# Loading x in one transfer per 256-token chunk, without VectorE's wait ahead of the statistics

## The reference, cut to what matters

```python
def bitlinear(x, W):
    sw = jnp.mean(jnp.abs(W)) + 1e-05
    Wq = jnp.clip(jnp.round(W / sw), -1.0, 1.0) * sw
    sx = 127.0 / jnp.clip(jnp.max(jnp.abs(x), axis=-1, keepdims=True), 1e-05, None)
    xq = jnp.clip(jnp.round(x * sx), -128.0, 127.0) / sx
    return jnp.einsum('bsd,od->bso', xq, Wq)
...
xn = _layernorm(x, axis=-1)
# attention: q (16 heads of 128), k and v (4 heads) by bitlinear, rope on q and k,
# causal softmax, output by bitlinear
x = x + attn(xn, Wq, Wk, Wv, Wo) + ffn(xn, gate_w, up_w, down_w, gate_s, up_s, down_s)
```

## Time and profile before

| | us |
|---|---|
| the two runs shown | 5373.88 and 5649.85 |
| their median | 5511.86 |
| the profiled execution | 5373.28 |
| span of its slowest core (core 2), first to last instruction | 5371.7 |
| spans of its eight cores | 5334.6 to 5371.7 |

### The profile page before, as it was taken

How to read it: one execution, slowest core, us unless ns; L and a number is a source line. 1 busy time by engine, 2 the same in 40 slices (tenths; PEclk the granted TensorE clock), 3 DMA queues, 4 the chain that set the end, 5 groups by cost and what they waited for, 6 DMA issues and landing times.

```text
span 5371.7 us, 55820 instructions; the slowest of 8 cores (5334.6 to 5371.7 us)
## 1 busy us (share of the span) xinstructions
PE 3815.0 (71%) x18728; PEld 1766.5 (33%) x18728; DVE 1706.2 (32%) x2837; ACT 1637.1 (30%) x1375; POOL 303.1 (6%) x276
## 2 busy tenths in 40 slices
PE   1799998979999898144445044545788989993188
PEld 1344444434444344133333033433222222222133
DVE  4211110111100000455555465665422111117533
ACT  4211110001111000533332622121455656663521
POOL 0111110101111010000000000000000000000000
PEclk9999999989999999566667576778999999995589
DMA  4999999999988697311110501101000000000366
GB/s 131 82 112 109 115 99 106 118 106 113 112 79 78 65 99 97 116 53 53 51 53 16 149 32 47 50 32 50 14 10 8 8 7 6 6 5 0 102 192 208
DMA packets 1048274, 387.69 MB, mean 72 GB/s; under 512 B 882240, under 2 KB 1025984, under 8 KB 1035712
## 3 DMA queue, kind: packets, MB, share of 16 engines
q0 software_dynamic: 548608, 161.50, 29.8%
q1 hardware_dynamic: 499392, 222.62, 18.3%
HBM read 480.53 MB, written 41.94 MB: 97 GB/s over the span
## 4 chain that ended last, share of the span: by engine, by line
PE 53%; DVE 19%; DMA 13%; ACT 9%; issue 5%; DVEq 1%; SPq 0%; ACTq 0%; POOLq 0%; POOL 0%
PE f_pd_h L389 10%; PE f_pg_h L343 9%; PE f_pu_h L349 8%; PE e_po L1018 4%; PE c_pse L811 3%; PE c_ppv L815 3%; ACT c_pp L869 2%; PE c_psc L860 2%; PE c_psc L858 2%; PE c_pse L813 2%; PE c_ppv L817 2%; PE b_pkv L625 2%; DVE b_mx L169 2%; DMA pp_wb<-wv_t 2%; DVE c_pp L878 2%
## 5 line engine op out<-in xcount | busy, mean ns | idle before, releaser
L869 ACT ACTIVATE c_pp<-c_psc 128x1024 bf16<-128x1024 f32 x640 | 654.7, 1023 | 583.8 <-PE c_psc L860 583.8
L343 PE MATMUL f_pg_h<-xnT,f_gw_h 128*128 128x512 bf16 x2816 | 628.5, 382 | 56.4 <-DMA f_uw_h<-uw_t 50.5
L389 PE MATMUL f_pd_h<-hdnT,f_dw_h 128*128 128x512 bf16 x2816 | 616.7, 381 | 46.4 <-DMA f_dw_h<-dw_t 44.1
L349 PE MATMUL f_pu_h<-xnT,f_uw_h 128*128 128x512 bf16 x2816 | 622.1, 379 | 0.0
L878 DVE TENSOR_TENSOR c_pp<-c_pp,cmask 128x512 bf16<-128x512 bf16 x512 | 217.8, 425 | 798.8 <-ACT c_pp L869 769.9
L726 PE MATMUL b_pq<-b_xqT,qtern 128*128 128x256 bf16 x2048 | 277.0, 297 | 244.6 <-DVE b_qrot L735 235.9
L343 PEld LDWEIGHTS f_pg_h<-xnT,f_gw_h 128*128 128x128 bf16 x2816 | 276.7, 98 | 394.1 <-issue 66.9
L389 PEld LDWEIGHTS f_pd_h<-hdnT,f_dw_h 128*128 128x128 bf16 x2816 | 275.9, 98 | 376.7 <-issue 53.4
L349 PEld LDWEIGHTS f_pu_h<-xnT,f_uw_h 128*128 128x128 bf16 x2816 | 275.5, 98 | 332.3
L603 PE MATMUL b_pkv<-b_xqT,ktern 128*128 128x256 bf16 x1024 | 180.9, 359 | 285.8 <-DVE b_krot L612 269.0
L811 PE MATMUL c_pse<-c_pp,c_onehot 128*16 128x512 bf16 x640 | 245.0, 383 | 133.9 <-DVE c_pp L878 127.7
(11 more groups left out here) (160 smaller groups left out, 3588.8 us busy)
## 6 DMA issues: line engine op xcount, KB each, us to landing
f_gw_h<-gw_t POOLq DMA_DIRECT2D x88, 512.0 KB, 9.2
f_uw_h<-uw_t POOLq DMA_DIRECT2D x88, 512.0 KB, 13.4
f_dw_h<-dw_t POOLq DMA_DIRECT2D x32, 1408.0 KB, 18.9
b_xch<-x_kv SPq DMA_DIRECT2D x32, 1024.0 KB, 6.8
f_xch<-x_q SPq DMA_DIRECT2D x4, 4096.0 KB, 17.0
pp_wb<-wq_t SPq DMA_DIRECT2D x64, 256.0 KB, 12.0
ffn_scr<-f_ffs_h SPq DMA_DIRECT2D x32, 512.0 KB, 5.1
pp_wb<-wo_t SPq DMA_DIRECT2D x64, 256.0 KB, 12.0
```

The costliest lines, as they stand in the source:

```text
L343: e.matmul(pg[:, bi, tc * 512:(tc + 1) * 512], gwb[wb][:, dt, :], xnT[:, dt, half * HT + tc * 512: half * HT + (tc + 1) * 512], start=(dt ...
L349: e.matmul(pu[:, bi, tc * 512:(tc + 1) * 512], uwb[wb][:, dt, :], xnT[:, dt, half * HT + tc * 512: half * HT + (tc + 1) * 512], start=(dt ...
L389: e.matmul(pd[:, pb, tc * 512:(tc + 1) * 512], dwb[wb][:, it, :], hdnT[:, it, tc * 512:(tc + 1) * 512], start=(it == 0), stop=(it == NIT - 1))
L869: E("scalar", lambda e, k0=k0, sbk=sbk: e.activation(pp[:, (k0 % 8):(k0 % 8) + 2, :].rearrange("p a b -> p (a b)"), psc[sbk][:], AF.Exp, s ...
```

## The change

For each chunk of B1 and B2 the two loads of 128 rows become one load of 256 rows into both halves of the tile, with one semaphore, for which both row sums and both sums of squares wait. The semaphores of the second halves go, and `emit_ln` takes one wait for all its tiles (stage F did so before). VectorE's separate wait for `xqT_pe[0]` ahead of the statistics goes too. Bytes moved, buffers and all arithmetic stay.

```diff
--- before.py
+++ after.py
@@ -82,8 +82,6 @@
     s_const = sem("s_const")
     s_x = [sem("s_x0"), sem("s_x1")]
     s_xb = [sem("s_xb0"), sem("s_xb1"), sem("s_xb2")]
-    s_xc = [sem("s_xc0"), sem("s_xc1"), sem("s_xc2")]
-    s_x2 = [sem("s_x20"), sem("s_x21")]
     s_rope = [sem("s_rope0"), sem("s_rope1")]
     s_mask = sem("s_mask")
     s_wb = [sem("s_wb0"), sem("s_wb1")]
@@ -134,14 +132,13 @@
 
     def emit_ln(xch, stats, wait_load, per_tile_fn=None):
         nt = stats["nt"]
-        wl = wait_load if isinstance(wait_load, list) else [wait_load] * nt
         sm, ssq_, mmean, rstd, nbias = (stats[k] for k in ("sm", "ssq", "m", "rstd", "nb"))
         for t in range(nt):
             E("vector", lambda e, t=t: e.reduce_sum(sm[:, t:t + 1], xch[:, t, :], AX.X),
-              waits=[wl[t], (ve, ve.n)], inc=(ve, 1))
+              waits=[wait_load, (ve, ve.n)], inc=(ve, 1))
             E("scalar", lambda e, t=t: e.activation(stats["junk"][:], xch[:, t, :],
                                                     AF.Square, accum_out=ssq_[:, t:t + 1]),
-              waits=[wl[t], (ac, ac.n)], inc=(ac, 1))
+              waits=[wait_load, (ac, ac.n)], inc=(ac, 1))
         vw, aw = ve.n, ac.n
         E("vector", lambda e: e.tensor_scalar(mmean[:], sm[:], 1.0 / D, None, ALU.mult),
           waits=[(ve, vw), (ac, aw)], inc=(ve, 1))
@@ -551,15 +548,11 @@
                 for c in range(NCH):
                     cb = c % 2
                     cb3 = c % 3
-                    ldw0 = (s_xb[cb3], s_xb[cb3].n + 16)
-                    ldw1 = (s_xc[cb3], s_xc[cb3].n + 16)
-                    ldw = [ldw0, ldw1]
+                    ldw = (s_xb[cb3], s_xb[cb3].n + 16)
                     E("sync", lambda e, c=c, cb3=cb3: e.dma_start(
-                        out=xch[:, cb3, 0, :], in_=x_kv[c * 256:c * 256 + 128, :]),
+                        out=xch[:, cb3, :, :], in_=x_kv[c * 256:(c + 1) * 256, :]
+                        .rearrange("(t p) f -> p t f", p=128)),
                       waits=[(ve, xch_done[cb3][0]), (ac, xch_done[cb3][1])], inc=(s_xb[cb3], 16))
-                    E("sync", lambda e, c=c, cb3=cb3: e.dma_start(
-                        out=xch[:, cb3, 1, :], in_=x_kv[c * 256 + 128:(c + 1) * 256, :]),
-                      waits=[(ve, xch_done[cb3][0]), (ac, xch_done[cb3][1])], inc=(s_xc[cb3], 16))
                     E("gpsimd", lambda e, c=c, cb=cb: e.dma_start(
                         out=ccks[:, cb, :], in_=cck[:, c * 256:(c + 1) * 256]),
                       waits=[(ve, rope_done[cb])], inc=(s_rope[cb], 16))
@@ -568,7 +561,6 @@
                       waits=[(ve, rope_done[cb])], inc=(s_rope[cb], 16))
                     RTOK = (s_rope[cb], s_rope[cb].n)
 
-                    E("vector", None, waits=[(pe, xqT_pe[0])])
                     stat_done = emit_ln(xch[:, cb3, :, :], stats, ldw)
                     round_acs = []
                     for t in range(2):
@@ -674,15 +666,11 @@
                 pend = [None]
                 for c in range(8):
                     cb = c % 2
-                    ldw0 = (s_x[cb], s_x[cb].n + 16)
-                    ldw1 = (s_x2[cb], s_x2[cb].n + 16)
-                    ldw = [ldw0, ldw1]
+                    ldw = (s_x[cb], s_x[cb].n + 16)
                     E("sync", lambda e, c=c: e.dma_start(
-                        out=xch[:, 0, 0, :], in_=x_q[c * 256:c * 256 + 128, :]),
+                        out=xch[:, 0, :, :], in_=x_q[c * 256:(c + 1) * 256, :]
+                        .rearrange("(t p) f -> p t f", p=128)),
                       waits=[(ve, xch_done[0][0]), (ac, xch_done[0][1])], inc=(s_x[cb], 16))
-                    E("sync", lambda e, c=c: e.dma_start(
-                        out=xch[:, 0, 1, :], in_=x_q[c * 256 + 128:(c + 1) * 256, :]),
-                      waits=[(ve, xch_done[0][0]), (ac, xch_done[0][1])], inc=(s_x2[cb], 16))
                     E("gpsimd", lambda e, c=c, cb=cb: e.dma_start(
                         out=ccqs[:, cb, :], in_=ccq[:, c * 256:(c + 1) * 256]),
                       waits=[(ve, rope_done[cb])], inc=(s_rope[cb], 16))
```

## The result

The changed kernel takes 1.0044 times as long as the one before (95% interval 1.0029 to 1.0059), which is 16 to 32 us of 5373. The forecast was + 21.5 us, 1.0040. A second comparison of the same two kernels gave 1.0053 (1.001 to 1.0095).

The account below looks back on a forecast made before the run. B1 and B2 were taken as chains hopping between engines, with B2's x load exposed. Wait 0, sums + 19.1 + 2.4, landing 0 made + 21.5 us on 5373.3, so 5394.8 us; own range 5380 to 5414, 5376 to 5424 for 8 in 10.

Parts of the forecast that it names:

- the 2% that I named: Whole kernel: a change under 2% taken as about indistinguishable from none; within 2% given 0.96, slower 0.03, faster 0.01.
- The wait at 0: B1 and B2: VectorE's wait for TensorE before the statistics is always already met, so removing it gains 0.
- my bound of 0.1 us a chunk: B1 and B2: most that removing VectorE's wait was to gain per chunk, 2.4 us over 24 chunks.
- The sums: Row sums lose overlap with the second half's landing, 2.39 us a chunk: 19.1 us in B2, 2.4 in B1's first chunk.
- The landing at 0: Exposed x loads: the merged 2 MB load lands 8.5 us after the first issue, as now, a difference of 0.
- the straight line: Load landing, interpolated between 1 MB (6.7 us) and 4 MB (17.0 us) loads: 2 MB at 10.1 us, 14.4 us lost.
- My bounds: Whole kernel: range 5380 to 5414 us, the sum less 4.4 and 2.4, plus 14.4, and some 6 us either side.
- Rival A: Exposed x loads: merged load lands up to 2.57 us sooner, giving 23.1 us back, 5371.7 us in all; chance 0.08.
- The saving of one fixed start: x loads: by the skill's estimate, one 2.0 us fixed part saved per merged load, 18 us, about 5377 in all.
- Rival B: Exposed x loads: merged load lands as late as the slowest 4 MB one, 28.7 us, total 5577 us; chance 0.05.
- My sign for it: x loads: a landing over 10.1 us by the issue rows would show the forecast wrong in favour of B.
- Rival C: VectorE's wait was real, 6.4 us in B2's chunk 5 and 0.1 in others; sum 5386 us; chance 0.04.
- the step on the median: Whole kernel: forecast is for an undisturbed run; a far-apart pair would lift a median some 138 us, not forecastable.

Follow-up runs that it names:

- e3: The changed kernel (one load) with VectorE's wait put back ahead of the statistics; stage B2 671.7 us against 671.3, B1 750.0 against 748.8.
- e5: The kernel before (two loads, wait kept) with the next chunk's loads issued early in B2, after ScalarE's normalisation; ratio 0.9911, B2 609.2 us.
- e1: The kernel before with only VectorE's wait ahead of the statistics removed in B1 and B2, two loads kept; ratio 1.0017, B2 650.7 us.
- e2: The kernel before without VectorE's wait, two loads kept, both halves' sums and squares waiting for both loads; ratio 1.0112, repeated 1.0037; B2 669.7 us.
- e6: The changed kernel (one load, no wait) with the next chunk's load issued early in B2; ratio 0.9896, B2 611.1 us.

## Why the sum was right, and where the prediction failed

*The size and the sign.* The sum was + 21.5 us. The ratio gives 16 to 32, and the stages give 20.4 + 1.4 = 21.8 us in the mean of the cores. That the sum and the stages agree to 0.3 us is partly luck: the landing was put too low by 0.6 to 1.9 us and the gain from the wait by some 1.0 us, and these errors nearly cancel (both are worked out below). The interval of the ratio is 0.15% to either side, so a change well under the 2% that I named could be told from none here.

*The wait at 0.* Right for B2 with the late issue, shown by taking it out alone (650.7 against 650.9 us) and by putting it back (671.7 against 671.3). It is not quite 0 where x is already there. From the mean of B1's first chunk to the first load of wq_t, means of the eight cores, the three kernels that have the wait take 735.0 (before), 735.1 (e3) and 735.0 us (e5); the five without it take 733.9 (changed), 734.3 (e1), 734.1 (e2), 734.0 (e6) and 733.7 us (the changed kernel once more). So the removal gave back some 1.0 us over B1's 15 further chunks, inside my bound of 0.1 us a chunk. The total of e1's B1 hides it, because the mean of its first chunk came 0.7 us later than in the kernel before (13.2 against 12.5 us after the first issue). In B2 the early issue points the same way: from the first mean to the load of the mask e5, which has the wait, takes 596.6 us and e6, which has not, 595.7, but these two differ in the form of the load as well. Which operations the removal shortens was not found, since the sum starts 0.11 us behind the copy with the wait and without.

*The sums.* 19.1 us were foretold for B2. Two loads with joint waits, which differ from before in this alone (the wait being worth nothing in B2), cost 18.8 us. For B1's first chunk I had 2.4 us, and there it is: its mean came 12.5 us after the first issue and comes 14.9 us after it in the changed kernel, 2.4 later. The stage grew by only 1.4, because the missing wait gives back 1.0 behind that. The 15 covered chunks pay nothing for their sums, as said.

*The landing at 0.* Slightly too low. The engines start 8.74 us after the issue where they started 8.50 us after the first of two, over all 64 loads of the eight cores; two loads with joint waits stay at 8.52. The other kernels with one load and the late issue have 8.70 (e3) and 8.62 (the changed kernel once more), those with two 8.55 (e1). So one load of 2 MB lands 0.1 to 0.2 us later than two of 1 MB issued 0.49 us apart, 0.6 to 1.9 us in eight chunks. That is inside my bounds of - 0.49 and + 1.6 us a chunk, and far from the 10.1 us of the straight line. My reason for 0 was in part luck: half of the 17.0 us of a 4 MB load is 8.5, but landings here are not in proportion to size. After the first megabyte, 4.9 to 6.4 us, each further one at 2.48 us would bring 4 MB after 12 to 14 us (an estimate from B2's loads), not 17.0.

My bounds, added as I described them, give 5382 to 5415 us and not 5380 to 5414; nothing hangs on it.

*Rival A* needed a landing under 6.1 us; the shortest in the changed kernel's B2 is 7.64. The saving of one fixed start does not appear at all: two loads in one queue already share it. The Trainium skill's *DMA: Bandwidth & Descriptors* makes that start 2.0 us in its section on the anatomy of one DMA, for single transfers that GpSimd issues; the loads here are SP's and follow each other, and one of 2 MB took 8.7 us where the page's formula gives 6.8. *Rival B* needed 18 us; the longest is 12.03. My sign for it, a landing over 10.1 us, did show in B2's first chunk (10.75 us in the mean of the cores), but it proves nothing for B: the same chunk takes 10.13 us with the two loads of before and up to 12.04 with those of e2. *Rival C* fell with e1.

*What was wrong* is the step on the median. I wrote that a pair of runs as far apart as the two shown "would again lift a median by some 138 us", and put that lift at 0 in the forecast of 5394.8 and in the range of 5376 to 5424 us. The median over all 14 runs is 5627.82, outside the range, and the lift is 227 us over the profiled 5400.7; the sentence on it in the result says where it comes from. No term of the sum is at fault: the profiled execution lies in the range. The lift differs from one comparison to the next for one and the same kernel: the kernel before has medians of 5373.42, 5436.64, 5634.4 and 5404.02 in the four, and the changed kernel 5627.82 and then 5545.23. The range should have reached at least as high as the 5649.85 of the two runs shown. Whether the change has any part in how often such runs come was not tried and stays open.

The slowest core's span grew by 27.5 us, more than the mean's 20.7. Two different cores are compared there: of the 27.5 us B1 and B2 hold 20.8, stage F 3.8 (core 0 reached the first load of wk_t at 2143.7 us, where core 2 before reached it at 2139.9), and the other stretches 2.9.

## What to carry to other kernels

In this kernel splitting the load paid where an engine stood waiting for it and could work on the first piece; the gain was that piece's work, one row sum of 2.39 us a chunk, and where the load was covered it was nothing. Fewer and larger transfers bought nothing, because back to back in one queue two loads of 1 MB stream like one of 2 MB. But the larger loss was the buffer freed too late. In chunk 4 of the kernel before its last reader, ScalarE's normalisation, ended at 3345.2 us, and the next load went out at 3400.3:

```profile
3343.12 2.09 ACT L699 ACTIVATE b_xn<-b_xch,b_nb,b_rstd 128x2048 f32<-128x2048 f32 x1
...
3400.27 0.33 SPq L680 DMA_DIRECT2D b_xch<-x_q  x1
```

Issuing it in that gap gave 41.7 us, twice what splitting or merging decides.

## What the runs showed of the hardware that was not expected

Back to back, the second megabyte lands 2.48 us behind the first, or 423 GB/s for one core, while the first takes 4.9 to 6.4 us (means of the eight cores for chunks 1 to 7 of B2 in the kernel before; in chunk 0 the second lands 4.5 us behind the first). That first part depends on the chunk in a fixed pattern: in the kernel before, the whole of x has arrived after 7.5 to 7.7 us in chunks 2, 4 and 7 and after 8.7 to 8.8 us in chunks 1, 3, 5 and 6 (means of the eight cores), and e1, e2, e3 and the changed kernel have the same chunks short and long. One load in place of two costs 0.3 to 0.4 us in the short ones and under 0.2 in the long ones. What sets the pattern was not tried.
